# Who writes the high half of V: ScalarE from the projection's PSUM bank instead of GpSimd from the staging tile

## What is computed

```python
x = x + attn_a(layernorm(x))      # 32 heads of 32 columns, softmax, output projection
x = x + ffn(layernorm(x))
x = x + attn_b(layernorm(x))      # 4 heads, sigmoid, causal
x = x + ffn(layernorm(x))

# attn_a, per batch of 512 rows
qkv = x @ attn_qkvw + attn_qkvb
scores = einsum('bhqd,bhkd->bhqk', q, k) / sqrt(32)
ctx = einsum('bhqk,bhkd->bhqd', softmax(scores), v)
```

## Time and profile before

| | us |
|---|---|
| median of 3 runs | 4112.76 |
| the profiled execution | 4105.42 |
| its span | 4103.7 |
| TensorE busy (matmul) | 3384.3 (82%) |
| VectorE busy | 2508.4 (61%) |
| GpSimd busy | 1817.6 (44%) |
| ScalarE busy | 1697.2 (41%) |

### The profile page before, as it was taken

How to read it: one execution, slowest core, us unless ns; L and a number is a source line. 1 busy time by engine, 2 the same in 40 slices (tenths; PEclk the granted TensorE clock), 3 DMA queues, 4 the chain that set the end, 5 groups by cost and what they waited for, 6 DMA issues and landing times. The chain is left out here.

```text
span 4103.7 us, 66460 instructions
## 1 busy us (share of the span) xinstructions
PE 3384.3 (82%) x24856; PEld 1745.7 (43%) x24856; DVE 2508.4 (61%) x4402; ACT 1697.2 (41%) x2180; POOL 1817.6 (44%) x1737
## 2 busy tenths in 40 slices
PE   0889889899898898988995688884988788865999
PEld 0344444344444443444443344452444444442444
DVE  7356667667566675676776555546566666654222
ACT  2256556566565565655665211111233333340000
POOL 2466666667667667666664233331232222220000
PEclk9999999999999999999998799997999998986999
DMA  5111221211211212122112433333112222214443
GB/s 169 31 48 45 56 46 42 60 40 47 55 46 47 51 50 51 38 58 47 41 34 90 159 134 123 128 133 142 65 70 83 83 83 81 82 50 161 150 150 122
DMA packets 265556, 327.38 MB, mean 80 GB/s; under 512 B 99904, under 2 KB 214592, under 8 KB 263872
## 3 DMA queue, kind: packets, MB, share of 16 engines
q1 hardware_dynamic: 260608, 306.84, 23.5%
q10 hardware_dynamic: 4608, 16.78, 1.0%
q0 software_dynamic: 64, 0.01, 0.0%
HBM read 151.53 MB, written 104.86 MB: 62 GB/s over the span
## 5 line engine op out<-in xcount | busy, mean ns | idle before, releaser
L633 DVE TENSOR_REDUCE nmax<-ring_ps 128x1 f32<-128x512 f32 x1024 | 684.9, 686 | 361.7 <-PE ring_ps L502 339.5
L559 PE MATMUL proj_ps<-xnT,wqk 128*128 128x512 f16 x3072 | 788.1, 395 | 119.4 <-DMA xnT<-v_sb 99.0
L592 ACT ACTIVATE e<-st_ps,exp_scale 128x1024 f32<-128x1024 f32 x512 | 570.9, 1115 | 502.9 <-PE st_ps L522 311.6
L721 POOL TENSOR_TENSOR elo<-e,ehi 128x1024 f16<-128x1024 f32 x256 | 609.3, 2380 | 319.9 <-ACT ehi L594 319.7
L594 ACT ACTIVATE ehi<-st_ps,exp_scale 128x1024 f16<-128x1024 f32 x512 | 570.3, 1114 | 193.6 <-PE ctx_ps L542 193.5
L559 PEld LDWEIGHTS proj_ps<-xnT,wqk 128*128 128x128 f16 x3072 | 300.5, 101 | 532.5 <-issue 153.4
L539 PE MATMUL ctx_ps<-v_sb,ehi 128*128 128x65 f16 x4096 | 379.4, 194 | 105.1 <-DVE sums L666 99.8
L522 PE MATMUL st_ps<-qs,ks 98*128 98x512 f16 x1024 | 400.5, 391 | 72.0 <-ACT ehi L594 71.9
L539 PEld LDWEIGHTS ctx_ps<-v_sb,ehi 128*128 128x128 f16 x4096 | 303.7, 99 | 255.6 <-DVE sums L666 142.9
L1274 PE MATMUL f_ps<-wm,fxT 128*128 128x512 f16 x1536 | 366.4, 395 | 43.7 <-DVE x L1485 28.5
L502 PE MATMUL ring_ps<-ks,qs 96*128 96x512 f16 x1024 | 395.3, 386 | 1.8 <-DVE nmax L633 1.5
(11 more groups left out here) (206 smaller groups left out, 4585.0 us busy)
## 6 DMA issues: line engine op xcount, KB each, us to landing
x<-x_scratch SPq DMA_DIRECT2D x64, 512.0 KB, 4.4
qs<-qk_hl SPq DMA_DIRECT2D x768, 32.0 KB, 1.9
ks<-qk_hl SPq DMA_DIRECT2D x768, 32.0 KB, 1.9
ctx_scratch<-ctx SPq DMA_DIRECT2D x64, 256.0 KB, 2.3
ct<-ctx_scratch SPq DMA_DIRECT2D x32, 512.0 KB, 4.0
xb<-in_L_attn_a_x_dram SPq DMA_DIRECT2D x32, 512.0 KB, 5.2
x_scratch<-ct SPq DMA_DIRECT2D x32, 512.0 KB, 5.6
xT_scratch<-xT SPq DMA_DIRECT2D x32, 512.0 KB, 2.6
```

The costliest lines, as they stand in the source:

```text
L559: mm = pe.matmul(proj_ps[:], wqk[:, wp, c, H * qk + P * g:H * qk + P * g + P], xnT[:, b % 2, xp, c, :], start=(n == 0), stop=(n == 23))
L592: nc.scalar.activation(e32[:, half], st_ps[:, half], ACT.Exp, scale=exp_scale[:, 0:1]).then_inc(e32_done, 1)
L633: dve.tensor_reduce(nmax[:, h % 2, c:c + 1], ring_ps[:, ring_max(h, c) % 2, :], AX.X, ALU.max, negate=True).then_inc(ring_free, 1)
L721: nc.gpsimd.tensor_tensor(elo[:, h % 2, 2:4, :], e32[:, 1], ehi[:, h % 2, 2:4, :], ALU.subtract).then_inc(elo_pool, 1)
```

## The change

ScalarE writes V's high half itself, straight from `proj_ps`, and then makes the float32 copy that raises `proj_free`. GpSimd drops its cast for V units and only subtracts. The wait that protects `v_sb` moves from GpSimd to ScalarE. For QK units nothing changes but the count in one wait. The values are the same.

```diff
@@ leave(u), ScalarE
                             else:
+                                b, t, half = u[1:]
+                                if t == 0:
+                                    if b == 0:
+                                        act.wait_ge(const_done, 4)
+                                    else:
+                                        act.wait_ge(pv_done, 2 * (HEADS_A * (b - 1) + 16 * half + 16))
+                                nc.scalar.activation(v_sb[:, t, 16 * half:16 * half + 16, 0:HD],
+                                                     proj_ps[:].rearrange("p (h d) -> p h d", d=HD), ACT.Copy)
                                 nc.scalar.activation(stage[:, i % 2], proj_ps[:], ACT.Copy).then_inc(proj_free, 1)
@@ split(u), GpSimd
                                 hi, lo = v_sb[:, t, heads, 0:HD], v_sb[:, t, heads, HD + 1:V1]
-                                if t == 0:
-                                    if b == 0:
-                                        pool.wait_ge(const_done, 4)
-                                    else:
-                                        pool.wait_ge(pv_done, 2 * (HEADS_A * (b - 1) + 16 * half + 16))
                             pool.wait_ge(proj_free, i + 1)
-                            nc.gpsimd.tensor_copy(hi, src).then_inc(hi_done, 1)
-                            pool.wait_ge(hi_done, i + 1)
+                            if u[0] == "QK":
+                                nc.gpsimd.tensor_copy(hi, src).then_inc(hi_done, 1)
+                                pool.wait_ge(hi_done, sum(v[0] == "QK" for v in order[:i + 1]))
                             nc.gpsimd.tensor_tensor(lo, src, hi, ALU.subtract).then_inc(split_done, 1)
```

## The result

The changed kernel takes 4128.01 us, the median of 7 runs (4119.58 to 4132.25), against 4113.86 us for the kernel before in the same comparison (7 runs): a ratio of 1.0033, 95% interval 1.002 to 1.0047. It is 8 to 19 us slower; the medians are 14.2 us apart. That is just over what can be told from no change.

The account below looks back on a forecast made before the run. Plain groups were taken to be paced by TensorE, tile groups by a loop of GpSimd and SyncE. 6.0 + 3.4 + 0 + 1.5 = 10.9 us slower than the 4112.76 us median: 4123.7 us, range 4108 to 4133.

Parts of the forecast that it names:

- The price of 0.49 us: ScalarE's added copy in front of `proj_free`: each one delays the bank's release by 0.49 us, ends 0.48 and 0.59.
- The estimate of 0.52: The same ScalarE copy priced by the Trainium skill's formula: 0.52 us each, for a sum of 12.0 us.
- Plain groups, 25 × 0.24 = 6.0 us: V units of g = 5, 6, 7 and the last batch's g = 0..3: 0.49 less 0.25 us given back, 6.0 us slower.
- The reason for the give-back: At L512 in plain groups: TensorE's 0.25 us wait for VectorE vanishes, as GpSimd's earlier subtraction lets VectorE's end 0.2 us earlier.
- g = 4, 7 × 0.49 = 3.4 us: V units of the first group behind the tile groups: no later wait absorbs the copy, 3.4 us slower.
- Tile groups, 0: 28 V units in groups paced by the GpSimd and SyncE loop: the queue's 21 us hide the copy, 0 us.
- the cast's removal, 0: GpSimd loses 64 casts, 45 us of work, outside the tile loop and not awaited in plain groups: worth 0.
- Rivals B: Tile groups pay too, if a later exponential gates their loop: 13.7 us added, 24.6 us slower, 4137; chance 0.08.
- C (19.9 us less): GpSimd's cast is in the tile groups' loop: 19.9 us off, 10.9 added, 4104; chance 0.10.
- Prologue, 1.5 us: Eight units back to back at the start: three V units with another behind them pay 0.49 us each, 1.5 us slower.
- Rival A: At the L512 wait VectorE is late too, nothing is given back: 17.2 us slower, 4130; chance 0.18.
- Rival D: The copy is hidden in plain groups as well, only the prologue's 1.5 us are left: 4114; chance 0.10.

Follow-up runs that it names:

- kernel 1: Kernel before, plus one more 16-bit ScalarE copy of the bank ahead of each V unit's release, GpSimd's cast kept; 4128.55 us.
- Kernels 4 and 10: 4: changed kernel, bank freed first, high half made from staging tile, 4103.75 us; 10: kernel before, GpSimd's V split waits for VectorE's sums, 4112.46 us.
- kernels 7 and 9: 7: kernel before, only the 7 V units of g = 4 changed, 4115.64 us; 9: changed kernel, those 7 units as before, 4122.76 us.
- kernels 5 and 2: 5: kernel before, only the 28 tile-group V units changed, 4112.08 us; 2: changed kernel without ScalarE's high-half copy, 4111.39 us.

## Why the prediction was right, point by point

**The direction and the mechanism.** "Any later `proj_free` is a later TensorE" is what the runs show: 0.33, 0.82 and 1.31 us of waiting for none, one and two copies, and the bank freed first takes the loss away with the same work on ScalarE. The price of 0.49 us was right. The estimate of 0.52 worked out from the Trainium skill ("ScalarE: Activation LUTs", What ACT_TABLE_LOAD costs) was too high by 0.03.

**Plain groups, 25 × 0.24 = 6.0 us.** Measured 0.17 us a unit (29.33 against 29.16), so 4 us. The wait that was to take up part of the delay did so, at each of the 25 units. So 0.32 of the 0.49 us came back instead of 0.25: 0.28 on the way to L512 (3.64 less 3.36), and 0.04 further on, which I didn't trace.

**The reason for the give-back** was wrong in one step: "With the cast gone, L777 starts right at `proj_free`, near 1166.02 instead of 1166.25, and L657 should end some 0.2 us earlier." L665 was stretched as before, to 2.07 us, and kernel 1 gets the same distance with the cast in place. TensorE's lateness alone uses up the wait. The Trainium skill ("SBUF — State Buffer", SBUF: two separate sides) says of a VectorE operation with two SBUF inputs and a GpSimd operation that reads SBUF that whichever starts first gets the shared pair of ports for the whole instruction, and the other blocks. Kernels 4 and 10 agree: 0.10 and 0.21 us of lead keep VectorE's subtraction at 1.22 us. I had used the contention and not the order.

**g = 4, 7 × 0.49 = 3.4 us.** The times of kernels 7 and 9 allow it (5.7 and 3.6 us by the medians); the traces say 2 to 8 us at equal time at 1.2 GHz, and up to 10.6 with the clock left aside. The term left out that TensorE's clock can stand at 1.2 GHz longer there. It is the term most likely too small; its size stays open.

**Tile groups, 0**, and **the cast's removal, 0**: both measured, in kernels 5 and 2, as nothing that the times can tell. Rivals B (13.7 us more) and C (19.9 us less) fall. **Prologue, 1.5 us:** from the first to the last of its four staging copies it is 22.10 us instead of 20.85, 1.25 us more. The first V unit behind it starts at 191.58 instead of 190.10, but that start lies anywhere from 188.25 to 190.49 in traces with the prologue of before, so it is weak evidence.

**The sum.** 10.9 us forecast, 14.2 measured, interval 8 to 19. With 4 for the plain groups and 1.5 for the prologue, 9 us are left for g = 4 and for what the intervals can't tell from nothing. So the plain term was 2 us too large, and by the medians some 5 us were missing beside it; that the sum came out near is in part luck. The stated range of 4108 to 4133 speaks little for it either, as it also took in rivals A (4130) and D (4114). It is the distances that decide between them. Rival A had no give-back, 17.2 us in all and plain groups at 29.6 us; they are 29.33 us apart, and TensorE's waits for VectorE at L512 fell from 49 to 20 between 180 and 2160 us. Rival D had them unchanged, at 29.16 us.

## What to carry to other kernels

Count what stands in front of a release, not what an engine has free: ScalarE was 41% busy, and still a 0.6 us copy ahead of `proj_free` cost TensorE 0.49 us each time. Freeing the bank first and working from the staged copy left TensorE's wait as it was. It also made this kernel 8 us faster, but for another reason: GpSimd's subtraction now started behind VectorE's. When work leaves an engine, look at what starts earlier in its place and whom it now meets.

## Not expected of the hardware

Which of VectorE and GpSimd started a subtraction 0.1 us earlier decided which of them was held up, for nearly the length of the other's operation: 1.22 and 2.10 us in one order, 2.07 and 1.13 in the other. It also held for a tiny VectorE operation (128x4), which took 1.01 us instead of 0.17 behind a GpSimd start 0.14 us earlier. So removing GpSimd's cast, 45 us of work, changed nothing, and delaying it by one wait in the plain groups saved 7 us.
